# Decoder layer on one core: clears moved behind the first normalisations, one late row turned in the step before, codes and two row pairs loaded sooner

## The reference

```python
x = x + attn(layernorm(x), Wq, bq, Wk, bk, Wv, bv)      # 32 query heads over 16 key heads of 32, causal
x = x + xattn(layernorm(x), ctx, ctx, mask)             # 64 context rows, 8 key heads, no projection
x = x + ffn(layernorm(x), gate, up, down)               # silu(x Wg^T) * (x Wu^T), then Wd^T; 3584 wide
# layernorm: (x - mean) / sqrt(var + 1e-5)
# Wg, Wu, Wd: 4 bit codes, looked up in a table of 16 values, times one scale for each block of 64
```

## Time and profile before

| | |
|---|---|
| median of 3 runs | 2630.06 us (2616.86 to 2631.15) |
| profiled execution | 2630.97 us |
| its span, first to last instruction | 2629.2 us |
| TensorE busy | 2450.1 us (93%) |
| VectorE, ScalarE, GpSimd busy | 1793.5, 1638.1, 1523.6 us (68%, 62%, 58%) |
| mean granted clock of TensorE | 0.965 |
| read from and written to memory | 192.81 MB, 73.40 MB |

### The profile page before, as it was taken

The page is one execution under the profiler, slowest core; times in us unless marked ns, Lnnn a source line. Parts: engine busy times, 40 slices in busy tenths (PEclk is TensorE's granted clock), DMA queues, the critical chain, the costliest instruction groups (busy, mean ns, idle before and its releaser), DMA issues.

```text
span 2629.2 us, 48595 instructions
## 1 busy us (share of the span) xinstructions
PE 2450.1 (93%) x17864; PEld 1340.4 (51%) x17864; DVE 1793.5 (68%) x3004; ACT 1638.1 (62%) x2998; POOL 1523.6 (58%) x1360
## 2 busy tenths in 40 slices
PE   6999999999986457999999999999999999999999
PEld 3566777777764343444444444444444444444444
DVE  6656678767777786777777777777777897646311
ACT  4466666666666446777777777777777686545200
POOL 2456667767778576777777777777767443212100
PEclk9999999999997558999999999999999999999999
DMA  6343443432322311222222222222223844323232
GB/s 204 99 147 93 122 132 100 130 108 88 104 86 72 88 64 49 92 90 84 81 90 85 83 93 89 92 90 89 85 82 100 268 136 144 113 96 105 70 105 78
DMA packets 225885, 271.11 MB, mean 103 GB/s; under 512 B 37616, under 2 KB 148720, under 8 KB 225648
## 3 DMA queue, kind: packets, MB, share of 16 engines
q1 hardware_dynamic: 225648, 268.00, 32.7%
HBM read 192.81 MB, written 73.40 MB: 101 GB/s over the span
## 4 chain that ended last, share of the span: by engine, by line
PE 50%; POOL 3%; issue 2%; DVE 2%; ACT 1%; DMA 1%; SPq 0%; DVEq 0%; ACTq 0%; POOLq 0%
PE ps L2135 29%; PE ps L2168 21%; POOL q_rows L500 1%; POOL xT L470 1%; POOL p L481 1%; POOL xn L2042 1%; DVE p L449 0%; ACT w_l L439 0%; DVE ps L449 0%; DMA h_parts<-xn 0%; POOL x_row L2048 0%; DVE xT L464 0%; DMA proj<-in_codes 0%; ACT q_rows L496 0%; ACT ps L436 0%
## 5 line engine op out<-in xcount | busy, mean ns | idle before, releaser
L449 DVE TENSOR_TENSOR ps<-ps,w_l 128x512 f32<-128x512 f32 x672 | 444.2, 693 | 237.4 <-ACT w_l L439 162.3
L1001 POOL TENSOR_TENSOR arena<-p,arena 128x512 f16<-128x512 f32 x320 | 370.7, 1167 | 229.8 <-ACT arena L1463 229.1
L470 POOL TENSOR_TENSOR xT<-xT,nat 128x512 f32<-128x512 f32 x162 | 206.3, 1274 | 451.1 <-DVE xT L464 451.1
L439 ACT ACTIVATE w_l<-proj 128x512 f32<-128x512 int32 x672 | 398.8, 618 | 64.2 <-DVE ps L449 52.2
L1455 ACT ACTIVATE p<-ps 128x512 f32<-128x512 f32 x320 | 191.1, 597 | 268.2 <-PE ps L1244 263.3
L1678 DVE TENSOR_REDUCE block_max<-ps 128x4 f32<-128x512 f32 x320 | 219.0, 688 | 179.1 <-PE ps L1215 176.2
L436 ACT ACTIVATE ps<-proj,small 128x512 f32<-128x512 int32 x336 | 217.7, 680 | 170.7 <-DVE xT L464 167.7
L2135 PE MATMUL ps<-arena,q_rows 128*128 128x512 f16 x1344 | 296.4, 380 | 5.6 <-DVE x_row L2315 3.8
L2395 DVE SCALAR_TENSOR_TENSOR arena<-ps,arena 128x1024 f32<-128x1024 f32 x70 | 85.1, 1221 | 211.4 <-PE ps L2168 208.9
L1185 PE MATMUL ps<-xT,w_h 128*128 128x512 f16 x720 | 219.3, 387 | 1.5 <-DVE xT L1632 1.5
L2135 PEld LDWEIGHTS ps<-arena,q_rows 128*128 128x128 f16 x1344 | 131.7, 98 | 165.9 <-issue 6.7
(11 more groups left out here) (249 smaller groups left out, 5949.0 us busy)
## 6 DMA issues: line engine op xcount, KB each, us to landing
proj<-in_codes SPq DMA_DIRECT2D x168, 256.0 KB, 2.9
nat<-in_scales SPq DMA_DIRECT2D x336, 128.0 KB, 2.9
h_parts<-xn SPq DMA_DIRECT2D x112, 256.0 KB, 2.3
nat_parts<-nat SPq DMA_DIRECT2D x48, 256.0 KB, 2.0
q_rows<-nat_parts SPq DMA_DIRECT2D x96, 128.0 KB, 2.8
w_l<-h_parts SPq DMA_DIRECT2D x21, 448.0 KB, 4.1
x_unit<-in_x SPq DMA_DIRECT2D x64, 128.0 KB, 2.7
x<-x_unit SPq DMA_DIRECT2D x64, 128.0 KB, 2.4
```

The costliest lines, as they stand in the source:

```text
L439: op = self.nc.scalar.activation(out, self.t.codes[:, t % 2, :], ACT.Copy, scale=slope, bias=intercept)
L449: self.nc.vector.tensor_tensor(other if n == self.LUT - 2 else held, held, other, ALU.max).then_inc(self.lut, 1)
L470: self.nc.gpsimd.tensor_tensor(self.quarter(t), self.quarter(t), self.t.scales[:, t % 2, :], ALU.mult)\
L1001: nc.gpsimd.tensor_tensor(p_l[:, n % 2, k, :], p32[:, f % 3, :], p_h[:, n % 2, k, :], ALU.subtract).then_inc(p_low, 1)
```

## The change

- GpSimd waits for the fourth normalisation (`ln_xn` 4) before its eight clears.
- In the head VectorE takes the statistics of the next row block ahead of the normalisation of the one before.
- Block 0 of the last batch's cross attention is measured and normalised in step 66 and turned in step 67 (`TO - 1`), both halves in bank 5 (`T_BANK + 1`), instead of ahead of the late loop in banks 2 and 3. To make room, the late scores go to bank 0 and the late results to bank 4. In the late loop `x_score(48)` stands ahead of `x_weigh(47)`, `x_soft(48)` ahead of `x_out(47)` and `shift(48)` ahead of `add_cross(47)`.
- The codes of tiles 0 and 1 are loaded right behind `lay_keys(B - 1)` and wait for cut 25 (the fourth of pair 3) instead of 28; their scales stay where they were.
- The rows of pairs 6 and 7 are loaded ahead of the stores of blocks 2 and 3 of the last batch.

```diff
@@ -410,0 +411,4 @@
+        self.load_codes(sp, t)
+        self.load_scales(sp, t)
+
+    def load_codes(self, sp, t):
@@ -414 +418 @@
-            sp.wait_ge(self.x_low, 7 * self.SET)
+            sp.wait_ge(self.x_low, 7 * (self.SET - 1) + 4)
@@ -418,0 +423,6 @@
+
+    def load_scales(self, sp, t):
+        chunk, kind, half = self.tile_at(t)
+        cols = slice(HALF * half, HALF * half + HALF)
+        if t == 0:
+            sp.wait_ge(self.x_low, 7 * self.SET)
@@ -666,0 +677,2 @@
+        if s == TO - 1:
+            return "cross", B - 1, 0
@@ -686 +698 @@
-        return PROJ_BANK + 1 - s % 2
+        return T_BANK + 1 if s == TO - 1 else PROJ_BANK + 1 - s % 2
@@ -691,2 +703 @@
-    LATE_ROWS = [(("cross", B - 1, 0), (-2, -2, None)), (("cross", B - 1, 1), (-1, 0, 1)),
-                 (("cross", B - 1, 2), (2, 3, 4)), (("cross", B - 1, 3), (4, 5, 6))]
+    LATE_ROWS = [(("cross", B - 1, 1), (-1, 0, 1)), (("cross", B - 1, 2), (2, 3, 4)), (("cross", B - 1, 3), (4, 5, 6))]
@@ -694 +705 @@
-    LATE_SLOTS = {at: n % 2 for n, (at, turns) in enumerate(LATE_ROWS)}
+    LATE_SLOTS = {("cross", B - 1, i): i % 2 for i in range(QT)}
@@ -708 +719 @@
-    LS_BANK, LT_BANK, LO_BANK, LN_BANK = 4, 5, 0, 1
+    LS_BANK, LT_BANK, LO_BANK, LN_BANK = 0, 5, 4, 1
@@ -962,0 +974,2 @@
+        for k in range(2):
+            feed.load_codes(sp, k)
@@ -975,2 +988,3 @@
-        for k in range(3):
-            feed.load_tile(sp, k)
+        for k in range(2):
+            feed.load_scales(sp, k)
+        feed.load_tile(sp, 2)
@@ -988,0 +1003 @@
+            feed.load_pair(sp, 4 + rt)
@@ -1076,0 +1092 @@
+        pool.wait_ge(ln_xn, 4)
@@ -1101,3 +1116,0 @@
-        ln_root(LN_AT["cross", B - 1, 0])
-        add_cross(LATE_X - 1, x_row[:, 1, :])
-        ln_root(LN_AT["cross", B - 1, 1])
@@ -1104,0 +1118 @@
+        ln_root(LN_AT["cross", B - 1, 1])
@@ -1108,0 +1123,2 @@
+            if n == 0:
+                add_cross(LATE_X - 1, x_row[:, 1, :])
@@ -1124 +1140 @@
-        turned_in = {PROJ_BANK: 0, PROJ_BANK + 1: 0, LN_BANK: 0}
+        turned_in = {PROJ_BANK: 0, PROJ_BANK + 1: 0, LN_BANK: 0, T_BANK + 1: 0}
@@ -1332 +1348,2 @@
-                    ln_turn(at, k // 2, turn_bank(s), (kind_read(min(s - 1 - FROM, NP * B - 1 - (s + 1) % 2)),))
+                    free = (t_exp, CHUNKS * NS) if s == TO - 1 else kind_read(min(s - 1 - FROM, NP * B - 1 - (s + 1) % 2))
+                    ln_turn(at, k // 2, turn_bank(s), (free,))
@@ -1347,4 +1363,0 @@
-            for half in range(2):
-                ln_turn(LN_AT["cross", B - 1, 0], half, PROJ_BANK + half)
-            pe.wait_ge(x_read, LATE_X - 1)
-            x_weigh(LATE_X - 1, XO_BANK, px_h, px_l)
@@ -1358 +1371 @@
-                        pe.wait_ge(x_low, LATE_X)
+                        pe.wait_ge(maxed, CHUNKS * NS)
@@ -1361,0 +1375,3 @@
+                if n == 0:
+                    pe.wait_ge(x_read, LATE_X - 1)
+                    x_weigh(LATE_X - 1, XO_BANK, px_h, px_l)
@@ -1367,2 +1382,0 @@
-                    if n == 2:
-                        pe.wait_ge(maxed, CHUNKS * NS)
@@ -1409,0 +1424,2 @@
+            elif half == 0 and what == "cross" and b == B - 1:
+                act.wait_ge(proj_done, NP * B)
@@ -1553,4 +1568,0 @@
-            if n == 0:
-                act.wait_ge(proj_done, NP * B)
-                for half in range(2):
-                    ln_high_part(LN_AT["cross", B - 1, 0], half, PROJ_BANK + half, xT[:, 0, :, :, :])
@@ -1641 +1653 @@
-            if at in LATE_SLOTS and b == B - 1:
+            if what == "cross" and b == B - 1:
@@ -1781,2 +1793,4 @@
-        def row_normal(i):
-            row = xn[:, i, :] if i < 2 else x_row[:, i - 2, :]
+        def first_row(i):
+            return xn[:, i, :] if i < 2 else x_row[:, i - 2, :]
+
+        def row_stats(i):
@@ -1784,2 +1798 @@
-            ln_stats(i, row)
-            ln_normal(i, row)
+            ln_stats(i, first_row(i))
@@ -1786,0 +1800,5 @@
+        def row_normal(i):
+            ln_normal(i, first_row(i))
+
+        row_stats(0)
+        row_stats(1)
@@ -1787,0 +1806 @@
+        row_stats(2)
@@ -1789,3 +1808,5 @@
-        for i in range(2):
-            row_low(i)
-            row_normal(2 + i)
+        row_low(0)
+        row_stats(3)
+        row_normal(2)
+        row_low(1)
+        row_normal(3)
@@ -1808,2 +1828,0 @@
-                at = ("cross", B - 1, 0)
-                turn_stats(at)
@@ -1811,5 +1829,0 @@
-                ln_normal(LN_AT[at], turn_row(at))
-                x_out(LATE_X - 1, XO_BANK)
-            if n == 0:
-                for half in range(2):
-                    ln_low_part(LN_AT["cross", B - 1, 0], half, PROJ_BANK + half, xT[:, 0, :, :, :])
@@ -1821,0 +1836,2 @@
+            if n == 0:
+                x_out(LATE_X - 1, XO_BANK)
@@ -1997,2 +2012,0 @@
-        for j in range(6, 8):
-            feed.load_pair(sp, j)
```

More of the change, by code:

```diff
@@ L410, in load_tile @@
     def load_tile(self, sp, t):
+        self.load_codes(sp, t)
[5 more added lines that the diff above has]
+            sp.wait_ge(self.x_low, 7 * (self.SET - 1) + 4)
+        if t >= 2:
+            sp.wait_ge(self.lined, self.NL * (t - 1))
+        sp.dma_start(self.t.codes[:, t % 2, :], self.dram["codes"][chunk, kind, :, cols])\
+            .then_inc(self.codes_loaded[t % 2], 16)
+    def load_scales(self, sp, t):
         chunk, kind, half = self.tile_at(t)
@@ L414, in load_tile @@
             sp.wait_ge(self.x_low, 7 * self.SET)
-        if t >= 2:
-            sp.wait_ge(self.lined, self.NL * (t - 1))
-        sp.dma_start(self.t.codes[:, t % 2, :], self.dram["codes"][chunk, kind, :, cols])\
-            .then_inc(self.codes_loaded[t % 2], 16)
         if t >= 2:
@@ L1100, in _ @@
             step(s)
-        ln_root(LN_AT["cross", B - 1, 0])
-        add_cross(LATE_X - 1, x_row[:, 1, :])
+        pair_lows(TO, 0)
         ln_root(LN_AT["cross", B - 1, 1])
-        pair_lows(TO, 0)
         for n in range(NX + 3):
@@ L1779, in step @@
                 cut_context(b, i - 12)
+        def first_row(i):
+            return xn[:, i, :] if i < 2 else x_row[:, i - 2, :]
+        def row_stats(i):
+            dve.wait_ge((row_loaded, late_loaded)[i // 2][i % 2], 16)
+            ln_stats(i, first_row(i))
         def row_normal(i):
-            row = xn[:, i, :] if i < 2 else x_row[:, i - 2, :]
-            dve.wait_ge((row_loaded, late_loaded)[i // 2][i % 2], 16)
-            ln_stats(i, row)
-            ln_normal(i, row)
+            ln_normal(i, first_row(i))
+        row_stats(0)
+        row_stats(1)
         row_normal(0)
+        row_stats(2)
         row_normal(1)
-        for i in range(2):
-            row_low(i)
-            row_normal(2 + i)
+        row_low(0)
[3 more added lines that the diff above has]
+        row_normal(3)
         row_low(2)
```

## The result

The changed kernel takes **2608.28 us** (median of 7 runs, 2601.20 to 2612.30), the kernel before 2625.0 in its 7 runs beside them (2616.86 to 2631.15): a ratio of 0.9933 with a 95% interval of 0.9916 to 0.9951, so 0.67% or 17.6 us faster (12.9 to 22.0); the two medians alone are 16.7 apart. The spans differ by 22.0 (2629.2 and 2607.2).

A forecast was written before the change was run, and what follows sets the result against it. A TensorE-bound body, with a head of some 30 us and a seam of some 250 us that is a chain of waits between engines. 8.4 + 6.6 + 6.1 = 21.1 off 2630.97 gives 2609.9, by the median 2609.0; range 2594 to 2619.

The forecast's parts named there:

- the 0.88: Whole kernel: the chance given to being faster by over 0.5%, that is below 2616.9 us.
- Part 1: Head: statistics ahead and clears behind the fourth normalisation bring the last low part 8.4 us sooner; bounds 2.6 and 9.4.
- held through the whole run of clears: Head: GpSimd's clears hold the fourth normalisation at 7.18 us, until 0.55 after the last clear.
- The bound of 2.6 below: Head: the least gain, if the moved clears stopped VectorE's low parts for 5.8 us.
- The rule that was weighed there: Head: the port pair is held for one whole instruction, so one clear at most is lost; gain smaller by 4.9.
- Clears only share the blame: Head rival: all but 1.45 us has another cause; head 3.5, time 2614; 0.12 with the other form, low parts stopped.
- Parts 2 and 3: Seam: row turned early and codes sooner, first draw 8.5 sooner, 6.6 us remaining; bounds 3.4 and 8.5.
- the values as what is late next: Seam: the last values, landed 4.3 later at 896.7, hold `x_weigh(48)`, which would otherwise come at 891.6.
- The choice of 1.6 us for the early row's normalisation beside the cuts: Seam, step 66: beside GpSimd's low cuts the normalisation takes 1.6 us; two such took 3.20, one alone 0.81.
- Part 4: Feed-forward start: rows of pairs 6 and 7 loaded sooner remove VectorE's 6.19 us wait; 6.1 us, bounds 4.0 and 6.2.
- slower body by the clock: TensorE-bound body, rival: granted clock stays at its lower level longer; 60 us of it give 2639; chance 0.03.
- More than forecast: Seam, rival: fewer gaps bring the clock back sooner, another 5 to 10 us, 2601; chance 0.11.

The follow-up runs named there:

- e8: The changed kernel unaltered, timed again beside the kernel before: 2604.6 against 2625.63 us, ratio 0.9919.
- e2: The kernel before with only the head's statistics put ahead, clears in their old place: 2621.68 us, ratio 0.9976.
- e11: The changed kernel with five of the eight clears put ahead of the fourth normalisation: 2607.45 us, ratio 0.9926 to the kernel before.
- e10: The kernel before with its eight clears reordered, the four large ones first: 2627.33 us, ratio 1.0003.
- e1: The kernel before with only the eight clears put behind the fourth normalisation: 2621.09 against 2626.92 us, ratio 0.9977.
- e3: The kernel before with the row turned early and the codes sooner, nothing of head or pairs 6 and 7: 2622.46 against 2626.92 us.
- e5: The kernel before with only the row turned early, codes in their old queue place: 2623.96 against 2625.63 us, ratio 0.9997.
- e4: The kernel before with only the rows of pairs 6 and 7 loaded sooner: 2621.59 against 2626.92 us, ratio 0.9976.

## Why the prediction was right

**The number.** 2609.0 was forecast, 2608.28 measured, within 2594 to 2619, and faster by over 0.5% as the 0.88 had it. A part of the closeness is luck. The sum of 21.1 was subtracted from 2630.06, a median of three; in 7 to 35 runs the kernel before lies at 2625.0 to 2627.3. So the base was 5.1 too high against the 7 runs, and the gain too large by about as much, 21.1 where 17.6 was measured (16.7 between the medians); the two errors cancel. (e8, the same kernel timed once more, gave 21.3.) The sum was read from one execution that had a held head and a body of 836.52, where those here run from 831.5 to 838.5.

**Part 1, 8.4.** In the two traces 8.63, step by step as it was laid out (normalisation ending at 16.32 against 16.3, first projection at 21.23 against 21.5, low parts not stretched). The step that failed is the one on which the size rests: that the normalisation is held through the whole run of clears. That was one outcome of two, read from one trace. Where it occurs the part gives 8.6, otherwise 2.4. Nor are both edits needed for it: the statistics alone give 8.15 (e2). The bound of 2.6 below was set for another reason, clears that stop the low parts, and that didn't occur.

The rule that was weighed there fares accordingly. In e2 and e11 the normalisation lost one clear, and this is what the Trainium skill (SBUF — State Buffer, SBUF: two separate sides) says of a pair held for one instruction; in before and e10 it stood through eight, which by the prediction's reading of that rule, one clear at most, should not be. The measurements decide: both happen, and one instruction is no upper bound for the wait. The rival built on it ("Clears only share the blame", head 3.5) didn't come in either form: with the clears gone, all of the 7.18 goes but 0.81 (e1). Its 1.45 for one clear is a mean over the x4 row, which is three clears of some 1.8 and one of 0.54.

**Parts 2 and 3, 6.6.** 5.9 in after, 7.3 in e3. The chain ran as worked out: first late softmax 5.8 (forecast 5.6), draw 9.2 (8.5), the values as what is late next. The net differs by 0.7, and its term is the landing of the last value: 5.0 us behind its issue, where 4.3 was taken. The choice of 1.6 us for the early row's normalisation beside the cuts was exact (1.64). e5 confirms what the working implied and didn't price: without the codes, the early row loses 2.0.

**Part 4, 6.1.** 5.9 to 6.0, alone (e4) and with the rest.

**What wasn't there.** No slower body by the clock: its dip is as deep and as long as it was. No gain from a better clock either ("More than forecast"). The body lent 1.2 us, which is inside its wander.

## What to carry to other kernels

A long operation in one profile may be one outcome of two: where two engines that can block each other are released by the same event, profile the same code several times before pricing its removal. Cut the spans of all traces at events that every version has; here this gave parts of 3 to 8 us to some tenths, where the times have 3 to 4 us of uncertainty and the body wanders by 7. And when an edit moves work on a chain, ask for each queue what now stands ahead of the next thing wanted: the early row alone lost 2.0, with the codes it won 5.9 to 7.3, and the wait it left behind was worth another 2.2 to 3.8, by the traces, for one moved line.

## What the runs showed of the hardware

The same normalisation (128x1024, SBUF to SBUF) beside back-to-back GpSimd clears took 0.95 (two executions), 2.05 (two) or 7.17 to 7.18 (five), the first and the last from the same start (e5 and before). Each time it ended 0.54 or 0.55 us behind the end of a clear, the third, the fourth or the eighth, and in the seam 0.55 or 0.56 behind the shift or the addition. GpSimd pays too when it loses: one clear 0.54 more (2.34 for 1.80 in e2), the addition 1.20 for 0.72. In the new head its affine select of `mask_qk` took 1.27 beside VectorE's `cut_w`, where in before (at 25.82, no `cut_w` beside it) it took 0.29; e8's row:

```profile
23.75 1.27 POOL L1100 TENSOR_SCALAR_AFFINE_SELECT mask_qk<-mask_qk 128x128 bf16<-128x128 bf16 x1
```

VectorE's low parts, which read PSUM and write f16, were not stretched by clears in any execution (two in 1.27 or 1.28 beside them, in e1, e5 and after, as without).
